# Even-numbered stages ahead of the second score products, on two engines

## What is computed

```python
x = x + jnp.tanh(g_xattn[0]) * L0_xattn(layernorm(x), ctx)   # softmax(q k / 4) v, projected
x = x + jnp.tanh(g_ffn[0])   * L0_ffn(layernorm(x))          # sigmoid router, top 4 of 8 experts + 1 shared
x = x + jnp.tanh(g_xattn[1]) * L1_xattn(layernorm(x), ctx)   # scores clipped, mean of v if any NaN
x = x + jnp.tanh(g_ffn[1])   * L1_ffn(layernorm(x))          # top 2 of 8 experts, width 1024
```

## Time and profile before

| | us |
|---|---|
| median of 3 runs | 1027.91 |
| lowest and highest run | 1020.56, 1039.43 |
| the profiled execution | 1020.56 |
| its span, first to last instruction | 1018.7 |
| mean granted TensorE clock in it | 0.903 of full |

### The profile page before, as it was taken

How to read it: one execution, slowest core, us unless ns; L and a number is a source line. 1 busy time by engine, 2 the same in 40 slices (tenths; PEclk the granted TensorE clock), 3 DMA queues, 4 the chain that set the end, 5 groups by cost and what they waited for, 6 DMA issues and landing times.

```text
span 1018.7 us, 18031 instructions
## 1 busy us (share of the span) xinstructions
PE 903.4 (89%) x6385; PEld 735.6 (72%) x6385; DVE 748.5 (73%) x1494; ACT 486.2 (48%) x842; POOL 241.9 (24%) x390
## 2 busy tenths in 40 slices
PE   3578999999999998999888888975699999999995
PEld 2355777777776776677665555643699999999995
DVE  3445667777676768988878789757598888888872
ACT  2135544444534443434434444431376666776762
POOL 5011111020210000101010133320524444444433
PEclk9569899999999999999999766665599999999998
DMA  6967786056154263738374873421666677776642
GB/s 154 167 131 134 173 198 133 25 99 106 43 71 76 45 118 75 140 103 134 85 148 94 220 154 98 122 75 34 235 222 208 212 232 228 231 227 220 208 146 31
DMA packets 129866, 141.52 MB, mean 139 GB/s; under 512 B 12561, under 2 KB 122281, under 8 KB 129649
## 3 DMA queue, kind: packets, MB, share of 16 engines
q1 hardware_dynamic: 119296, 127.59, 51.2%
q0 software_dynamic: 8832, 12.25, 5.6%
q10 hardware_dynamic: 1648, 0.53, 0.2%
HBM read 109.45 MB, written 30.36 MB: 137 GB/s over the span
## 4 chain that ended last, share of the span: by engine, by line
PE 66%; DVE 21%; issue 5%; ACT 3%; POOL 2%; DMA 1%; POOLq 0%; DVEq 0%; ACTq 0%
PE bank L966 12%; PE bank L802 8%; PE by_query L950 7%; PE by_key L950 7%; DVE rowmax L1298 5%; PE bank L812 4%; PE value_bank L744 4%; PE bank L650 4%; PE by_query L707 3%; DVE probs L1323 3%; PE bank L693 3%; PE bank L771 2%; PE bank L659 2%; PE by_key L726 2%; DVE stats L1253 1%
## 5 line engine op out<-in xcount | busy, mean ns | idle before, releaser
L1102 ACT ACTIVATE probs<-by_key 128x1024 f32<-128x1024 f32 x128 | 130.7, 1021 | 92.2 <-PE by_key L726 91.4
L1298 DVE TENSOR_REDUCE rowmax<-by_query 128x4 f32<-128x1024 f32 x128 | 155.4, 1214 | 17.0 <-PE by_query L707 16.9
L1791 POOL TENSOR_SCALAR rstd<-moments 128x2 f32<-128x2 f32 x32 | 10.5, 328 | 514.9 <-DVE moments L1257 514.9
L1851 POOL DMA_INDIRECT out_x<-x,token_i x46 | 78.0, 1695 | 146.8 <-ACT x L1208 139.8
L966 PE MATMUL bank<-w_hi,h_hi 128*128 128x256 f32 x368 | 104.1, 283 | 0.0
L966 PE MATMUL bank<-w_lo,h_hi 128*128 128x256 f32 x368 | 104.1, 283 | 0.0
L966 PE MATMUL bank<-w_hi,h_lo 128*128 128x256 f32 x368 | 104.1, 283 | 0.0
L707 PE MATMUL by_query<-stack_k,stack_q 48*128 48x256 f32 x512 | 70.9, 358 | 35.6 <-DVE rowmax L1298 35.3
L707 PEld LDWEIGHTS by_query<-stack_k,stack_q 48*128 48x128 f32 x512 | 42.8, 206 | 76.7 <-DVE rowmax L1298 46.9
L744 PE MATMUL value_bank<-probs,values 128*32 128x256 f32 x1024 | 79.4, 433 | 8.9 <-DVE probs L1323 8.8
L812 PE MATMUL bank<-w_down,hidden 128*128 128x256 f32 x288 | 79.9, 401 | 3.7 <-DVE summed L1361 1.8
(11 more groups left out here) (242 smaller groups left out, 2147.7 us busy)
## 6 DMA issues: line engine op xcount, KB each, us to landing
w<-in_L_ffn_W SPq DMA_DIRECT2D x46, 1024.0 KB, 8.7
lower<-lower SPq DMA_DIRECT2D x64, 256.0 KB, 5.3
stack_k<-qk SPq DMA_DIRECT2D x96, 128.0 KB, 5.2
stack_q<-qk SPq DMA_DIRECT2D x96, 128.0 KB, 7.0
qk<-hi SPq DMA_DIRECT2D x31, 256.0 KB, 2.9
qk<-lo SPq DMA_DIRECT2D x31, 256.0 KB, 2.6
rows<-w_gate SPq DMA_DIRECT2D x8, 264.0 KB, 4.6
x<-in_x SPq DMA_DIRECT2D x8, 256.0 KB, 7.0
```

What stands on the lines that cost most here:

```text
L1102: ac.activation(probs[i % 4][:, :, :, :].rearrange("p k h s -> p h k s"), by_key[:, :, :].rearrange("p h (k s) -> p h k s", k=2), ACT.Exp) ...
L1298: dv.tensor_reduce(rowmax[u % 2][:, :, p, :], by_query[:, :, :].rearrange("p h (t s) -> p h t s", t=TT), AX, ALU.max).then_inc(sem.max_don ...
L1851: po.indirect_dma_start(out[:, :], bass.IndirectOffsetOnAxis(ap=token_i[:, n:n + 1].bitcast(U32), axis=0), ysb[i % 3][:, t, :], None, comp ...
```

## The change

On TensorE the even stages of a slot go ahead of scores_by_key. On ScalarE the even stages go ahead of the exponential of that slot. Nothing else differs.

```diff
@@ TensorE
             v, q = divmod(g - base(0), PAIRS)
             if 0 <= v < UNITS:
                 scores_by_query(v, q)
+            for stage, n in PLAN[2 * g]:
+                if stage in stages:
+                    stages[stage](n)
             u, p = divmod(g - base(0) - LAG, PAIRS)
             if 0 <= u < UNITS:
                 scores_by_key(u, p)
-            for stage, n in PLAN[2 * g]:
-                if stage in stages:
-                    stages[stage](n)
             u, p = divmod(g - base(0) - LAG - 3, PAIRS)
             if 0 <= u < UNITS and p % 2 == 0:
                 weigh_values(u, p // 2)
@@ ScalarE
         for g in range(SLOTS_IN_ALL):
-            for stage, n in PLAN[2 * g - 1]:
+            for stage, n in PLAN[2 * g - 1] + PLAN[2 * g]:
                 if stage in stages:
                     stages[stage](n)
             u, p = divmod(g - base(0) - LAG, PAIRS)
             if 0 <= u < UNITS:
                 exponentials(u, p)
-            for stage, n in PLAN[2 * g]:
-                if stage in stages:
-                    stages[stage](n)
```

## The result

The changed kernel is a little slower: 1033.19 us in the median of 20 runs against 1027.75 for the kernel before in 20 runs, ratio 1.0059 with a 95% interval of 1.0038 to 1.0081. That is +5.4 us, or +6.1 by the ratio, where +15 was forecast. The direction was right, the size was not.

What follows compares the result with a forecast made beforehand. TensorE was taken as the bound from 115 to 395 us. Drains on the path 19.5 us, plus 3 for late exponentials, less 7.5 gain, made +15 us: a median of 1043 us, range 1023 to 1062.

Steps and rivals of the forecast that it cites:

- The bound and the drains: TensorE bounds 115 to 395 us; parting by_query and by_key adds drains, 28.7 us at full clock, between 0 and 34.
- A price: TensorE slots with even work where weigh_values follows by_key: extra 0.20 us each, 32 slots make 6.4 us.
- C: TensorE, 6 slots with even work, neither weigh_values nor odd stages following: 1.01 us before and after, nothing extra.
- B slots: TensorE slots with even work where odd stages, not weigh_values, follow by_key: extra 0.53 us each, 42 make 22.3 us.
- What lies on the path: Drains that lengthen the kernel: 1.5 us (65-115), 12 (115-395), 4 (395-560), 2 (560-680), together 19.5 us.
- ScalarE's late exponentials: Finish slots 138, 143, 148, 155: exponential waits behind even copies, then next by_key waits; 3 us in all, 0 to 6.
- sign of being wrong: In the profile after, waits before by_key's loads (L726) for the exponential beyond 5 us would show the forecast wrong.
- The gain: ScalarE's even copies ahead of the exponential: 5 us, plus 2.5 from shorter maxima waits; 7.5 us, between 0 and 33.
- The sum: Whole kernel: 19.5 + 3 - 7.5 = +15 us, so a median of 1043 us.
- absorbed: Rival: drains fall where TensorE waits anyway, or by_key has no entry gap; -5 to +5 us, chance 0.17.
- The clock case: Rival: added gaps make the clock's fall at 560 us begin 40 us sooner; +20 on top of +15, 1063, chance 0.10.

Runs made afterwards that it cites:

- The pair with the short clip and maxima: Kernel before and changed kernel, both with VectorE's clip cut to 2 of 1024 columns and row maxima to 32 of 256: medians 973.5 and 984.0 us.

## Why the forecast was too high

**The bound and the drains.** Right. The entry of 0.33 us belongs to by_key as well; 41 such gaps stand in the stretch of layer 0 and 73 in the kernel. The rule of the Trainium skill that I weighed, that a change of the tiling mode empties TensorE (TensorEngine Tiling (Array Packing), Tiling Modes under Key Properties), holds for the pair that no trace had shown: the sum goes by 0.33 and not by nothing. The traces show the gap; what the array does in it they don't show. The A price of 0.20 is exact, and C costs nothing (slot 84, -0.01). The count is one too high: slot 100 has no even product on TensorE, and by_key still starts 0.23 us behind by_query there (425.43 and 425.66 in after). So there are 41 B slots, 10 of them in slots 97 to 127.

**The B price.** The term is mis-sized: 0.53 against 0.39. I took one exit and one entry from single rows and left out that the first full-array group behind an exit loads for 0.11 us less, although showed it (L771, eight loads in 1.59 us). Gross, at 0.39 for every B slot and so rather too high, slots 44 to 97 cost 3.2 + 9.0 = 12.2 us, not 15.4, and the whole 6.4 + 16.0 = 22.4 at full clock, not 28.7.

**What lies on the path.** This is the step that failed. I wrote that from 115 to 395 us TensorE is the bound, that some 3 us of waits shrink, and took 12 us. Measured in slots 44 to 97 is +4.5 us. From 12.2 gross, 7.7 came back: the waits of TensorE's loads for other engines fell from 19.5 to 11.1 us there. My 3 us for the maxima were about right (7.1 to 3.9 in these slots). What I had set against no drain are the other waits, for lo, hidden and x above all, 12.4 us before and 7.2 after; three of them, 3.0 us, I had taken for a gain instead. A busy share of 96% did not mean a loss that adds up over 280 us. Every few slots VectorE's chain sets the pace, and TensorE waits there, for 0.2 to 2.0 us. A drain in front of such a wait only makes it shorter. Slots 73 to 76 show it: the changed kernel loses 0.19, 0.35 and 0.19 us in three slots, and the wait for the maxima behind slot 76 is 0.81 us where it was 1.96. The difference of 1.15 is the 0.73 of the three slots and the price of slot 76 itself (0.39 where VectorE is freed). Before, then after:

```profile
283.45 0.84 PEld L812 LDWEIGHTS bank<-w_down,hidden 128*128 128x128 f32 x4
286.25 0.30 PEld L707 LDWEIGHTS by_query<-stack_k,stack_q 48*128 48x128 f32 x4 [1.96 <-DVE rowmax L1298]
```
```profile
294.21 0.73 PEld L812 LDWEIGHTS bank<-w_down,hidden 128*128 128x128 f32 x4
295.75 0.30 PEld L707 LDWEIGHTS by_query<-stack_k,stack_q 48*128 48x128 f32 x4 [0.81 <-DVE rowmax L1295]
```

I had compared the drains of the whole stretch with one entry of the waits, 7.1 us. The sum that counts goes from one wait to the next: the smaller of the drains lost since the last wait and the wait at the end, over all waits on any engine. Worked out from the trace of before, with 0.20 and 0.39 us as prices, it gives back 7.9 us in slots 44 to 97 (7.1 if 0.33 of each wait before by_query is taken for the drain), against 7.7 measured; in slots 97 to 128 it gives back 4.7 of 5.7. That is an estimate made with the result known, and it does not hold slot by slot: the wait for lo in slot 50 fell by 0.58 us (1.07 to 0.49), though drains of some 0.8 us (slots 48 and 50) stood before it. For layer 1 I took 4 of 7.6 us; by the slots that repeat it was between -0.1 and +0.3. The pair with the short clip and maxima shows that it is mostly VectorE that covers: 8.3 and 4.1 us come out when it is freed.

**ScalarE's late exponentials.** I put 3 us on four finish slots. What the traces show is elsewhere: by_key waits for the exponential for 2.6 us in the ramp (65 to 115 us, three times) and for 2.5 us behind 560 us (0.8 before). All such waits add up to 5.1 us, where 1.2 were before; I had named more than 5 us as a sign of being wrong. Whether the 3 us are right for the finish slots stays open, since slots behind 128 and before 44 differ by more than that between two executions of one program.

**The gain.** I took 7.5 us: 5 for copies ahead of the exponential and 2.5 for shorter waits for the maxima. The first was 0.9 us in slots 44 to 97, in the one slot that I had read, and I had stretched it over 16 units. The two waits for lo that I counted with it had another cause; ScalarE's move alone did not gain there. The second can't be told from the cover.

**The sum.** Located are +4.5 us in slots 44 to 97 and at most +0.3 in 97 to 128, of the measured 5.4. The last 0.6 to 1.0 us, less than the interval of the ratio is wide (3.9 to 8.3 us for the whole), lies where the traces don't repeat, before slot 44, behind 128 or in the four varying slots, and stays unplaced. The two errors had opposite signs: too little cover and too much gain (7.5 us, of which 0.9 is shown). The likeliest case should have been the one that I called absorbed, whose upper end was +5. The clock case did not happen: from 115 to 395 us the granted clock is 1.00 and from 395 to 560 us 0.98, in both kernels.

## What to carry to other kernels

Work that an engine gains or loses in small pieces need not add up over a stretch, even where its busy share is 96%: go from one wait on another engine to the next and take, each time, only what exceeds the wait at the end. Where no wait covers it, parting products that use the array in the same form costs time, and the price of parting them is read from the distance between starts of equal neighbours, drain and shorter first group together. Compare equal slots of two traces, not spans: here a stretch of 281 us repeats to 0.03 us while the ramp in front of it moves by 8 us.

## What the runs showed of the hardware

- The first full-array weight-load group behind a change of form takes 0.73 us for four loads, the following ones 0.84 (eight: 1.59 and 1.70). So a drain of 0.33 us costs 0.22 net of it.
- Two executions of one program entered slot 44 at 118.54 and 126.76 us, with a mean granted clock of 1.00 and 0.74 in the same 10 us of the ramp. The fastest and the slowest run of the kernel before lie 18.9 us apart (1020.56 and 1039.43 us); in the two traces such ramps make up 8.2 us. Behind the ramp the clock can fall in single slots, in one execution and not in the next: slot 117 took 6.39 and 9.22 us in the two traces of before, slot 120 11.11 and 9.42.
- Behind products of 8 columns the clock fell to the lower level in slot 64, 1.68 us lost, in both kernels with even stages behind weigh_values, and in none of the twelve other traces. The idle time before these products does not decide it: 0.95 and 0.82 us where it fell, 0.81 and 0.82 in the two traces of before, where it did not. Since each of the two kernels has one trace, and slots 117 and 120 differ between executions of one program, it is not shown that the order of the stages caused it, nor what decides it.
